# Attention input features: a transposing DMA of two f16 halves and a vector add, in place of matmuls and copies

## The reference

```python
h = inp @ W                                   # inp: relu(layernorm(x)), 4096 x 256
Wh1 = h @ a[:F_out, :]
Wh2 = h @ a[F_out:, :]
e = leaky_relu(Wh1 + Wh2.T, 0.2)
attention          =  softmax(where(adj > 0,  e, -1e12), axis=1)
negative_attention = -softmax(where(adj > 0, -e, -1e12), axis=1)
h_prime_double = concatenate([attention @ inp, negative_attention @ inp], axis=1)
x = x + elu(h_prime_double @ wtrans)
```

## Time and profile before

| | |
|---|---|
| three runs | 2407.91, 2411.95, 2412.57 us |
| span of the profiled execution (first to last instruction) | 2402.9 us |
| median less that span | 9.05 us |
| busy: PE, DVE, ACT, POOL | 2177.9, 1541.8, 1308.5, 112.0 us |
| mean granted TensorE clock | 0.975 |
| mean DMA rate over the span | 115 GB/s |
| the preparation of the attention (steps 1 to 5) | from about 1283 to 1370.5 us of the span |

### The profile page before, as it was taken

One profiled execution on the slowest core, in us unless ns is written; L12 is line 12 of the kernel. 1 busy time (PEld: TensorE's weight loads), 2 busy tenths in 40 slices (PEclk: granted clock), 3 DMA queues, 4 the chain that ended last, 5 costly groups with the idle time before them and its releaser, 6 DMA issues.

```text
span 2402.9 us, 31618 instructions
## 1 busy us (share of the span) xinstructions
PE 2177.9 (91%) x10873; PEld 1473.3 (61%) x10980; DVE 1541.8 (64%) x2723; ACT 1308.5 (54%) x1652; POOL 112.0 (5%) x54
## 2 busy tenths in 40 slices
PE   2664999999999999999998999999999999898998
PEld 1332555555554555555445477777777878787887
DVE  5776534400004323324447899999999999999886
ACT  6776465555556555556664354535454555445463
POOL 0000000000000000000000000201010100202020
PEclk9976999999999999999998999999999999999999
DMA  8997211300011011121125536153434434352400
GB/s 298 324 327 255 73 53 56 122 16 18 9 53 62 27 53 53 62 94 53 53 79 178 185 137 216 65 193 105 157 122 154 143 124 165 105 183 74 136 18 9
DMA packets 152954, 276.74 MB, mean 115 GB/s; under 512 B 6688, under 2 KB 79136, under 8 KB 144672
## 3 DMA queue, kind: packets, MB, share of 16 engines
q1 hardware_dynamic: 144416, 267.15, 33.3%
q10 hardware_dynamic: 8448, 8.39, 1.0%
HBM read 241.96 MB, written 33.55 MB: 115 GB/s over the span
## 4 chain that ended last, share of the span: by engine, by line
PE 56%; DVE 22%; issue 9%; DMA 6%; ACT 6%; DVEq 0%; SPq 0%; ACTq 0%; POOL 0%
PE ps L1233 34%; PE ps L1353 11%; PE ps L1258 8%; DVE work L1096 8%; DVE work L1107 5%; DMA work<-in_adj_t 5%; DVE feat L1017 3%; DVE feat L1013 3%; ACT big L436 2%; PE ps L1178 2%; ACT work L436 2%; ACT work L690 1%; DMA feat<-in_adj 1%; PE ps L1211 1%; PE ps L1243 1%
## 5 line engine op out<-in xcount | busy, mean ns | idle before, releaser
L1353 PE MATMUL ps<-big,work 128*128 128x257 f32 x4096 | 924.8, 385 | 67.6 <-ACT work L690 66.9
L1353 PEld LDWEIGHTS ps<-big,work 128*128 128x128 f32 x4096 | 774.7, 191 | 213.6 <-ACT work L690 102.1
L1233 PE MATMUL ps<-work,feat 128*128 128x512 bf16 x3687 | 815.9, 379 | 11.3 <-DVE feat L869 4.4
L1233 PEld LDWEIGHTS ps<-work,feat 128*128 128x128 f16 x3776 | 369.0, 98 | 446.8 <-issue 6.7
L436 ACT ACTIVATE work<-big 128x1024 bf16<-128x1024 uint8 (+1 forms) x472 | 495.9, 1054 | 257.3 <-PE ps L1233 253.3
L690 ACT ACTIVATE work<-work,feat 128x512 f32<-128x512 f32 x512 | 344.5, 714 | 501.2 <-DVE work L1107 498.4
L1096 DVE SCALAR_TENSOR_TENSOR work<-feat 128x512 f32<-128x512 f32 x512 | 429.8, 875 | 32.7 <-PE ps L1353 26.4
L1107 DVE TENSOR_TENSOR work<-big,work 128x1024 f32<-128x1024 f32 x256 | 323.8, 1270 | 0.0
L1258 PE MATMUL ps<-work 128*128 128x256 f32 x896 | 199.0, 379 | 4.5 <-ACT work L436 4.5
L1258 PEld LDWEIGHTS ps<-work 128*128 128x128 f32 x896 | 169.9, 190 | 32.0 <-ACT work L436 6.5
L900 DVE TENSOR_REDUCE gmax<-work 128x256 f32 (+1 forms) x32 | 11.8, 413 | 262.6 <-ACT work L539 262.6
(11 more groups left out here) (145 smaller groups left out, 1011.7 us busy)
## 6 DMA issues: line engine op xcount, KB each, us to landing
work<-in_adj_t SPq DMA_DIRECT2D x128, 512.0 KB, 5.3
big<-in_adj_t SPq DMA_DIRECT2D x64, 1024.0 KB, 5.6
feat<-in_adj SPq DMA_DIRECT2D x64, 1024.0 KB, 5.6
h_spill<-work SPq DMA_DIRECT2D x32, 512.0 KB, 4.1
feat<-h_spill SPq DMA_DIRECT2D x32, 512.0 KB, 4.3
x_spill<-work SPq DMA_DIRECT2D x24, 512.0 KB, 3.0
work<-in_x SPq DMA_DIRECT2D x16, 512.0 KB, 5.1
work<-x_spill SPq DMA_DIRECT2D x16, 512.0 KB, 4.1
```

The source lines that it names most:

```text
L1233: ins = mm(ps[:, bank + f, :], parts[:, j, h, f * P:(f + 1) * P], stage[:, g % STAGES, jj, :], start=(fresh and h == 0), stop=(end and h = ...
L1353: ins = mm(ps[:, 4 * s + t, 0:YW], E[:, j % RING, t * P:(t + 1) * P], Yb[:, j, s, :], start=(j == 0), stop=(j == NT - 1), skip_group_check ...
```

## The change

PE's `transposed` and ACT's `ht_copy` go. SP issues one DMA transpose for each chunk instead. It reads the chunk's 128 x 2048 f16 numbers (4 tiles, 2 halves, 256 features) and writes 16 blocks of 128 x 128 into one of four slots (`T_halves`), which lie in the memory of `h_ring` and `x_ring`. DVE adds the two halves of a chunk to f32 in `T_all` and signals `ht_evac`. Transposes 0 to 3 stand in SP's code behind the last reload, and in front of the wait for `uv_ready` and the load of `wtrans`; transposes 4 to 7 each wait until DVE has added the chunk whose slot they take, and stand in front of the four mask loads. The row loads wait for all transposes.

```diff
+        T_halves = words(work, 4096, RING * CH).bitcast(f16).rearrange("p (s t h k n) -> p s t h k n", s=4, t=TPC, h=2, k=FB)
...
+            def transpose_chunk(c):
+                sp.wait_ge(parts_in[c], 64)
+                if c >= 4:
+                    sp.wait_ge(ht_evac, c - 3)
+                sp.dma_start_transpose(T_halves[:, c % 4, :, :, :, :].rearrange("p t h k n -> p (t h k) n"),
+                                       parts[:, c * TPC:(c + 1) * TPC, :, :].rearrange("p j h f -> p (j h f)"))\
+                  .then_inc(halves_in[c % 4], 16)
+            for c in range(4):
+                transpose_chunk(c)
             sp.wait_ge(uv_ready, 1)
...
+            for c in range(4, NC):
+                transpose_chunk(c)
             sp.wait_ge(panel_ready, staged(4))
             for g in range(NC // 2):
                 load_mask(0, g)
-            sp.wait_ge(ht_ready, NC)
+            for s in range(4):
+                sp.wait_ge(halves_in[s], 32)
             for h in range(2):
                 load_row(0, h)
...
-            def ht_copy(c):
-                if c == 0:
-                    act.wait_ge(panel_ready, staged(4))
-                act.wait_ge(ht_ready, c + 1)
-                k = 2 * (c % 2)
-                copy(T_all[:, c, :, :], ps[:, k:k + 2, :]).then_inc(ht_evac, 1)
...
             ch.link(nc.vector.tensor_scalar(t_row, t_row, v_c1, v_r, ALU.subtract, ALU.mult))
             for c in range(NC):
+                if c == 0:
+                    dve.wait_ge(panel_ready, staged(4))
+                dve.wait_ge(halves_in[c % 4], 16 * (c // 4 + 1))
+                halves = T_halves[:, c % 4, :, :, :, :]
+                nc.vector.tensor_tensor(T_all[:, c, :, :].rearrange("p k (t n) -> p t k n", t=TPC),
+                                        halves[:, :, 0, :, :], halves[:, :, 1, :, :], ALU.add).then_inc(ht_evac, 1)
+            for c in range(NC):
                 dve.wait_ge(ht_evac, c + 1)
                 nc.vector.tensor_reduce(hsum[:, :, c:c + 1], T_all[:, c, :, :], AX.X, ALU.add).then_inc(ht_summed, 1)
...
-            def transposed(c):
-                ...
-            for c in range(EARLY):
-                transposed(c)
             pe.wait_ge(uv_ready, 1)
             for c in range(NC):
                 ...
-            for c in range(EARLY, NC):
-                transposed(c)
             pe.wait_ge(weights_in, W_NEEDED[4])
             pe.wait_ge(ht_evac, NC)
```

More of the change, by code:

```diff
@@ L173, in gnn_stack @@
         gown_ready, gall_ready = sem("gown_ready"), sem("gall_ready")
-        ht_ready, ht_evac, ht_summed = sem("ht_ready"), sem("ht_evac"), sem("ht_summed")
+        halves_in = [sem(f"halves_in{s}") for s in range(4)]
+        ht_evac, ht_summed = sem("ht_evac"), sem("ht_summed")
         y_ps_ready, y_evac, uv_ready, cols_ready = sem("y_ps_ready"), sem("y_evac"), sem("uv_ready"), sem("cols_ready")
@@ L612, in _ @@
                     stage_groups(0, 0, 4, l + 1)
-                if l == 3:
-                    ht_copy(0)
                 post_std(NC - 1)
@@ L620, in _ @@
                     copy(wa_rows, ps[:, 4, :].rearrange("p (s f) -> p s f", s=2)).then_inc(wa_rows_ready, 1)
-                if l == 3:
-                    ht_copy(1)
                 post(NC - 1, 1, H - 1, (0, 1))
@@ L626, in _ @@
                 post(NC - 1, 1, H - 1, (2, 3))
-            for c in range(2, EARLY):
-                ht_copy(c)
             act.wait_ge(out_ready, 4 * NT)
@@ L999, in _ @@
             nc.vector.tensor_reduce(hsum1[:, :], hsum[:, :, :], AX.X, ALU.add).then_inc(hsum_ready, 1)
-            dve.wait_ge(ht_ready, NC)
+            for s in range(4):
+                dve.wait_ge(halves_in[s], 32)
             nc.vector.tensor_copy(u_col, uv_sb[:, :, 0])
```

## The result

The changed kernel takes 2426.95 us (median of four runs, 2423.9 to 2430.74), the kernel before beside it 2410.55 us (four runs, 2407.91 to 2412.57): a ratio of 1.0073, 95% interval 1.0059 to 1.0088. That is 16.4 us slower; 21 were forecast.

A forecast was written before the change was run, and what follows sets the result against it. PE is busy 91% of the span, but locally PE and DVE join 2 us apart at 1366.38. Last addition at 1334.2 delays that by 21.2: span 2402.9 + 21.2 = 2424.1, plus 9.05 gives 2433 us; range 2424 to 2481, own 2428 to 2443.

The forecast's parts named there:

- the meeting: PE's spreading at tile 29, where PE's projections and DVE's row searches join: from 1366.38 to 1387.6, +21.2 us.
- the term d: One 512 KB transpose's share of the DMA queue's time: 3.0 us taken, 1.3 and 6.5 kept as bounds.
- 1310.2 + 8d: End of DVE's last addition, paced by eight transposes in the DMA queue: 1334.2 us.
- The slots don't hold this up: Transpose 4's wait for a free slot: ready by 1322.7, before its landing at 1324.0, so no delay.
- The straight line over pieces: Transpose price on the DMA queue from two packet sizes: 1.2 ns a piece, 2.0 ns a KB, 3.5 us.
- A - 1313.0: Delay where PE and DVE join at tile 29, for a last addition ending at A: +21.2 us.
- The clock: PE's projections start at the low clock after idling, near 0.55: +1.6 us.
- nothing changes: Attention after PE's spreading at tile 29 keeps its order, loads and waits: 1036.5 us to the end, within 2 us.
- Rival 1: DMA queue: a transpose costs the same as a plain load, 1.3 us; +12.9, 2425 us; chance 15%.
- Rival 2: DMA queue: small pieces bound each transpose, 4.2 to 9 us; 2461 us at 6.5, up to 2481; chance 20%.
- Rival 3: DMA transposes: 16 blocks of 128 x 128 go one after another, far above 9 us each; 2577 or near 2790; 10%.
- Rival 4: Attention's first chunk gives the delay back from 10.3 us of row-load waiting and issue; 2412 us; chance 3%.

The follow-up runs named there:

- additions alone: Changed kernel without any transposes, DVE's additions reading old feature halves: 2419.34 us, ratio 1.0052 to the kernel before.
- the controlled pair: Kernel with early transposes into eight slots plus useless PE matmuls before the projections, 224 against 290 of them: 2415.71 and 2412.03 us.
- the doubled kernel: Changed kernel with every transpose issued twice, the second into spare memory and also waited for: 2446.14 us.

## Why the prediction was right or wrong

**Where the 19.5 us at the meeting come from**, from the runs (U+):

| step | meeting | difference |
|---|---|---|
| before | 67.4 | |
| additions in front, transposes hidden, PE kept busy | 77.6 | 10.2 |
| PE idle, clock low (additions alone) | 79.8 | 2.3 |
| transposes in the queue (rows ahead of three masks) | 84.4 | 4.6 |
| masks ahead of the rows (the changed kernel) | 86.9 | 2.5 |

**Direction and mechanism: right.** All five marks were found in kind. (a) SP is held for each transpose; the pace is nonetheless the queue's, as the plain copies show; (b) four additions go back to back and four wait, 2.45 us apart instead of 3; (c) the clock is 0.50 after the idle time; (d) the first row search waits for the row load; (e) the delay is at the meeting, and from there to the end it is 1035.0 us instead of 1036.5.

**The additions: right.** 1.2 us was forecast for each, 1.22 to 1.23 was measured, and with transposes left out PE started at U+25.90, forecast 1325.3 - 1298.97 = 26.3. That this is more than half the loss stood in the prediction as a remark on DVE's place and not in its sum; the sum named the last addition only.

**The step that was off is the term d:** forecast 3.0 us, measured 2.4. The general form 1310.2 + 8d, which would take 4.8 us from the last addition, holds only while the queue is later than the slots. "The slots don't hold this up" was worked out for d = 3.0; with 2.4 the prediction's own rule for a slot gives 1316.8 + 2.9 + 2.4 = 1322.1 for transpose 4, the last addition at 1322.1 + 7.2 + 1.2 = 1330.5, U+31.5, and 3.7 us off the meeting. Measured are U+31.37 for the end of that addition and U+31.52 for PE's start, and the run with eight slots, where PE starts 1.6 us sooner, confirms the wait. So this part of the sum was sound, and its term d was mis-sized. The straight line over pieces gave 3.5, and the choice of 3.0 was a compromise. The measured prices are 0.6 ns a piece and some 2.4 ns a KB, where the line had 1.2 and 2.0: it was drawn through 3.2 and 5.2 ns, and an error of 0.2 ns in each is enough for that. Whether the 3.2 ns held the queue's start-up, as the prediction took it, no run shows. By the Trainium skill's 261 GB/s ("DMA: Bandwidth & Descriptors", Latency and other measured facts) the estimate is d = 2.0, too little here: the trace has 212 GB/s.

**The row loads: they bind, by more than was forecast.** The forecast had DVE and PE arrive within 0.1 us of each other, and its rule for the meeting, A - 1313.0, follows PE alone. The first row landed 15.2 us after the last transpose (1352.27 against 1337.03), not 13.3; so of the 3.9 us by which the transposes were early only 1.9 were left at the search, and DVE is 1.67 us later than PE at the meeting. Part of this shows in the rows. ACT has mask 0 at 1340.82, 3.8 us behind the last transpose instead of 2.7, and in the stretch of masks and row load the queue moved 361 GB/s and not 394:

```profile
1334.60:1352.00 17.40, 13.60 (x27) 6.03 (x28) 12.11 (x16) 5.38 (x7) 0.00 (x0) 0.78 1.03 361
```

Why it was slower was not tried.

**The clock:** forecast +1.6, measured +2.0 in the changed kernel and 2.3 in the controlled pair.

**Behind the meeting "nothing changes": off by 1.5 us, within the bound given.** The kernel before is the odd one: its spreading takes 3.01 us, behind a wait of 2.00, and the same stretch of before reads

```profile
1366.30:1369.40 3.10, 3.02 (x17) 3.05 (x18) 0.69 (x2) 0.00 (x0) 0.00 (x0) 0.64 0.75 296
```

with the granted clock at 0.64. All other kernels of this study have 2.02 us or less there, and 1034.3 to 1035.3 us from meeting to end. The 12 projecting matmuls behind the spreading take 6.03 us there and 5.32 in the others, so these two differences, 1.0 and 0.7 us, cover the 1.5. Only one execution of the kernel before was profiled, so that it may be the execution and not the kernel that is odd.

**The time around the span was mistaken.** The 9.05 us of the kernel before were not what lies around a span. For the changed kernel the profiled execution took 2430.74 us with a span of 2428.8, 1.9 us more, and the others are alike (2416.86 and 2415.1 for the additions alone). So the profiled execution of before was a quick one, some 2405 us. The sum survives, since only the difference was added to the median.

**How near the time came is partly luck.** From the forecast's 21.2 us, d takes 3.7, the late row loads add 2.0, the stretch behind the meeting takes 1.5 and the unexplained rest 1.6, which leaves the measured 16.4. The late row loads and the smaller d, both mistakes of the sum, work against each other. The 2428 of the estimate with d = 2.0 is near for the same reason.

**The rivals.** Rival 1 (a transpose is like a plain load, 2425) is nearer in time than the forecast (2433 against 2426.95) and still false: d is 2.4 and not 1.3, and at the meeting, 19.5 us late, its 12.9 are further off than the forecast's 21.2. Run as a kernel, by 4096-byte copies, it has its last addition at U+26.9 (forecast 1325.9, U+26.9) and its meeting 5.3 us before the changed kernel's. Rival 2 (the pieces bound it) names the right cause at too high a price. Rival 3 (blocks in sequence) is excluded: 16 blocks in 2.4 us are 0.15 us a block, and the Trainium skill's 1309 ns ("VectorE: DVE Perf Modes", The three transpose paths) isn't the pace of a transpose of many blocks. Rival 4 (given back behind the meeting) did not happen: 1.5 us, and no kernel showed more than 2.2. The chances differ by 0.01 between two places: 97% stands there as 0.96, and rival 4's 3% as 0.04.

## What to carry to other kernels

Taking work off PE is worth nothing where another engine sets the start. Here 128 matmuls and eight copies lay under DVE's row, and the addition that came in their place stands on DVE and costs 10 us even with transposes that are hidden, and 12.4 with the low clock behind PE's idle time. Price a DMA by its pieces (2048 of 256 bytes went at half the rate of 128 of 4096), not by its bytes or by the name of the operation, and look what is queued behind it: masks and row loads. A short form such as 1310.2 + 8d holds only while the same wait ends last. When a term of such a sum changes, go through the waits again that it covered (the slots here, and ACT's mask in the doubled kernel).

## What the runs showed of the hardware that was not expected

- A copy within the chip's memory ran at 215 GB/s in 256-byte pieces and 405 GB/s in 4096-byte pieces, with DMA shares of 0.96 and 1.01. The Trainium skill, "DMA: Bandwidth & Descriptors", Why small descriptors are slow (HBM only), says that such copies don't suffer from small pieces. These two runs differ from it.
- SP is held by the issue of a transpose (2.65 us on average in the first four) and by the issue of a plain copy in small pieces as well (8.59 us for the first four; 3.78 for four in 4096-byte pieces), so that all that is written behind waits.
- POOL's addition held back DVE's small instructions, with two inputs (L957) and with one (L940), until it was done: 0.4 us became 2.1 to 2.3. DVE's maxima and minima (0.67 to 0.69 us) were not held back.
- After 4.12 us without work the clock granted to PE was 0.50; after a wait of 1.67 us the spreading still went at its usual 2.02 us, and after one of 2.00 us, in the kernel before, it took 3.01 us at 0.64.
